# First expert stage in 64-slot tiles on quarters of the matrix array, its expert weights loaded in nine blocks each

## The chip, the core and the metric

The kernel runs on one NeuronCore of a Trainium2 chip. The core has TensorE (PE in the profile) for matrix products, VectorE (DVE), ScalarE (ACT), GpSimd (POOL) and SyncE (SP). In this kernel SP issues all plain transfers, and POOL issues the indirect ones (gather and scatter by row number). All run side by side and wait for each other through semaphores. The metric is the device time in microseconds (us), as the median of several runs.

## What is computed

A small vision tower over 16 images of 36 tokens, so 576 tokens of width 192, in float32. Patches are normalised and projected to tokens; then come an attention block, a first mixture of experts, a Mamba-style block with its own feed-forward part, and a second mixture of experts (top 2 of 8). The change is in the first mixture:

```python
route = softmax(x @ router_w + router_b)          # 576 tokens, 8 experts
max_prob, max_ind = route.max(), route.argmax()   # every token goes to one expert
for e in range(8):                                # w1, w2: 192x512   w3: 512x192
    oe = silu(xe @ w1[e]) * (xe @ w2[e]) @ w3[e]  # xe: the tokens of expert e
out = out.bfloat16 * max_prob
```

## The kernel before, in words

**Tiles of slots.** Tokens are sorted by expert on the chip. A tile is 128 slots that all belong to one expert. 576 tokens over 8 experts can need at most (576 + 8*127) // 128 = 12 tiles, so the program always runs 12 (`M1_TILES`). Tiles 0 to 7 are the first tile of experts 0 to 7; tiles 8 to 11 are the overflow, and belong to the expert that a table `te` names, which VectorE computes after routing. Each tile has its own weights: `wup` (w1 and w2, with the 192 input rows cut into 128 and 64) and `wdn` (w3). There are 8 weight buffers (`M1_BUFS`) for the first stage and 6 larger ones, in the same memory, for the second.

**Loading.** `expert_weights` on SP issues five transfers per tile: 96x1024, 32x1024, 64x512 and 64x512 elements into `wup`, 128x768 into `wdn` (lines 417 to 421). Experts 0 to 5 are issued during attention, then the token rows are written out (`token_rows`), then experts 6 and 7 and `later_experts` for the overflow tiles. Tile 8 waits for `v_te` and for the first tile's end (`p_y` counts the tiles finished by the down product), tile 9 for the second tile's end, and so on. For an overflow tile SP reads the expert number with `value_load` (line 440) and computes each source address.

**Computing.** For tile j TensorE runs `up_main` (K=128 rows of input: 8 products of 128x128x128, line 1604), `up_rest` (the remaining 64 input rows: 8 products in pairs, one on the upper and one on the lower half of the array's rows, line 1616), then `down(j-1)` (4 products of 128x128x192, line 1629). ScalarE applies silu (line 774), VectorE multiplies (line 1196), ScalarE copies the result (`result`, line 781), and POOL scatters it to `token_y` (line 604). Tokens come in by POOL's gather (`xg`, line 597) and are transposed on TensorE (line 1580). Only the first tile needs no gather: `first_tile` (line 1547) selects its tokens with a product by a 0/1 matrix. Next come `sources`, which finds the row numbers, and the gathers.

**After the stage.** SP waits for all scatters (line 445), then reads `yg` back, and VectorE adds it to `h`. The next block depends on this, so the end of the stage sets the start of all that follows.

## Time and profile before

| | before |
|---|---|
| time, median of 3 runs (lowest to highest) | 406.29 us (405.89 to 407.03) |
| profiled execution: its own time, its span | 409.78 us, 408.0 us |
| PE busy | 348.6 us (85%) |
| first expert stage, first up product to last down product | 119.5 to 180.2 us |
| TensorE products of the stage | 12 tiles of 20 |
| experts loaded during the stage | 4 (of 1,152 KB each) |

How to read it: times in the trace are us from the start of the span. A row of the chain of work is start, duration, engine and line, with the number of instructions. A timeline row is start, duration, engine, line, operation and operands, with the idle time before it in brackets. PE rows count two records for each float32 product of the program (8 products are "x16"), PEld is the weight load that goes with each, and "64*64" is the rows and columns of the array used. A row of the table of windows is the stretch, its length, then busy time and count for PE, PEld, DVE, ACT and POOL (only PE and PEld where one line was asked for), the granted TensorE clock (1.00 is 2.4 GHz, 0.50 is 1.2 GHz), the busy share of the DMA engines, and GB/s. "SPq" is a transfer being issued on SP; "us to landing" runs from issue to the last byte.

### The profile page before, as it was taken

Reading aid. Unit: us, or ns where it says so; the run is one execution under the profiler, and the core shown is the slowest. Engines: PE = TensorE matmul, PEld = TensorE weight load, DVE = VectorE, ACT = ScalarE, POOL = GpSimd, SP = SyncE. Lnnn points to the kernel's source line nnn. Section 1 sums busy time; section 2 is a strip of 40 time slices with the busy share of each in tenths; the row PEclk is TensorE's granted clock in tenths of the full one; section 3 lists DMA queues with packets and bytes.
Section 4 is the critical chain, followed back from the end, with each engine's and each line's share of the span. In section 5 each row is a group of like instructions: output and inputs, shape, how many; then the busy total and the mean of one; then the engine's idle time right before and its main releaser. Section 6 shows DMA issues by size and latency. Waiting matters only on the chain.

```text
span 408.0 us, 7081 instructions
## 1 busy us (share of the span) xinstructions
PE 348.6 (85%) x2758; PEld 291.5 (71%) x2758; DVE 184.0 (45%) x474; ACT 134.8 (33%) x278; POOL 104.5 (26%) x133
## 2 busy tenths in 40 slices
PE   4999946989788999966896987888899999999970
PEld 1999923567667999962465654575799999999960
DVE  2786793996552222216398555266422212121213
ACT  2997311444303222321387042321321212121210
POOL 3299542000023443122032202000423232211120
PEclk9999976987776999996999798995999999999995
DMA  7933239930371795007003999002249999999204
GB/s 237 345 84 75 63 81 253 271 93 2 108 202 52 203 247 124 15 16 195 0 0 77 258 252 259 28 0 67 60 105 291 277 254 255 258 251 249 65 31 130
DMA packets 28707, 59.51 MB, mean 146 GB/s; under 512 B 10081, under 2 KB 15234, under 8 KB 28674
## 3 DMA queue, kind: packets, MB, share of 16 engines
q1 hardware_dynamic: 26274, 53.48, 50.1%
q0 software_dynamic: 2400, 5.57, 5.0%
q8 instruction: 22, 0.36, 0.4%
q14 instruction: 11, 0.09, 0.1%
HBM read 55.12 MB, written 3.92 MB: 145 GB/s over the span
## 4 chain that ended last, share of the span: by engine, by line
PE 60%; DVE 17%; ACT 8%; DMA 8%; issue 4%; SPq 2%; POOL 0%; DVEq 0%; POOLq 0%; ACTq 0%
PE ps L1604 15%; PE ps L1629 12%; PE ps L1616 9%; PE ps L1412 4%; PE ps L1345 4%; DMA xw<-in_xw 3%; DVE cv L1264 3%; ACT xp L661 2%; PE ps L1418 2%; DVE xn L974 2%; DVE xn L950 2%; PE ps L1467 2%; SPq L349 2%; PE ps L1547 2%; DMA yg<-token_y 2%
## 5 line engine op out<-in xcount | busy, mean ns | idle before, releaser
L1604 PE MATMUL ps<-xgt,wup 128*128 128x128 f32 x576 | 70.9, 280 | 2.3 <-DVE ht L1196 1.8
L1604 PEld LDWEIGHTS ps<-xgt,wup 128*128 128x128 f32 x576 | 69.4, 196 | 2.8 <-issue 2.8
L1196 DVE TENSOR_TENSOR ht<-sg,ps 128x384 f32<-128x384 f32 (+1 forms) x56 | 27.7, 497 | 77.5 <-ACT sg L774 75.5
L597 POOL DMA_INDIRECT xg<-token_x,src_id x26 | 25.3, 972 | 145.5 <-DVE src_id L1166 95.3
L1629 PE MATMUL ps<-wdn,ht 128*128 128x192 f32 x288 | 53.8, 335 | 0.0
L1345 PE MATMUL ps<-busy 128*128 128x512 bf16 x108 | 38.9, 486 | 11.1 <-DVE h L1211 6.6
L1629 PEld LDWEIGHTS ps<-wdn,ht 128*128 128x128 f32 x288 | 46.1, 190 | 3.1
L604 POOL DMA_INDIRECT token_y<-ysb,row_id x28 | 27.5, 981 | 67.6 <-ACT ysb L781 67.6
L774 ACT ACTIVATE sg<-ps 128x384 f32<-128x384 f32 (+1 forms) x56 | 24.8, 444 | 49.9 <-PE ps L1616 49.1
L1353 PE MATMUL ps<-weff,xp 128*128 128x193 f32 x240 | 39.9, 327 | 1.6 <-ACT xp L661 1.6
L1353 PEld LDWEIGHTS ps<-weff,xp 128*128 128x128 f32 x240 | 39.2, 190 | 2.4 <-issue 2.4
L1616 PE MATMUL ps<-xgt,wup 64*128 64x128 f32 x576 | 40.5, 286 | 0.0
L1616 PEld LDWEIGHTS ps<-xgt,wup 64*128 64x128 f32 x576 | 35.0, 190 | 4.2 <-issue 2.5
L1190 DVE COPY xgt<-ps 128x256 f32<-128x256 f32 (+1 forms) x14 | 5.7, 405 | 49.2 <-PE ps L1580 49.2
L1345 PEld LDWEIGHTS ps<-busy 128*128 128x128 bf16 x108 | 11.9, 116 | 22.2 <-issue 8.3
L661 ACT COPY xp<-xw 128x576 f32<-128x576 f32 x24 | 16.0, 667 | 6.7 <-DMA xw<-in_xw 6.7
L770 ACT COPY xgt<-ps 128x256 f32<-128x256 f32 (+1 forms) x14 | 5.0, 357 | 38.4 <-PE ps L1580 38.4
L1388 PE MATMUL ps<-ident,xn 128*128 128x128 f32 x30 | 6.3, 301 | 10.9 <-DVE xn L950 8.9
L690 ACT ACTIVATE std<-mv,eps_t 128x1 f32<-128x1 f32 x20 | 5.9, 294 | 28.4 <-DVE mv L960 28.4
L1388 PEld LDWEIGHTS ps<-ident,xn 128*128 128x128 f32 x30 | 3.9, 149 | 15.0 <-DVE xn L950 10.6
L781 ACT COPY ysb<-ps 128x192 f32<-128x192 f32 x16 | 5.1, 318 | 26.3 <-PE ps L1629 26.3
L909 DVE TENSOR_REDUCE acc<-wall 128x192 f32<-128x3072 f32 (+1 forms) x2 | 10.5, 5236 | 5.3 <-ACT wall L674 3.8
(295 smaller groups left out, 511.0 us busy)
## 6 DMA issues: line engine op xcount, KB each, us to landing
wup<-in_m_w SPq DMA_DIRECT2D x16, 576.0 KB, 8.5
wup<-in_m_w SPq DMA_DIRECT2D x48, 192.0 KB, 9.4
wdn<-in_m_w SPq DMA_DIRECT2D x16, 576.0 KB, 11.4
wup<-in_m_w SPq DMA_DIRECT2D x12, 384.0 KB, 6.1
wup<-in_m_w SPq DMA_DIRECT2D x36, 128.0 KB, 6.6
wdn<-in_m_w SPq DMA_DIRECT2D x12, 384.0 KB, 9.3
xw<-in_xw SPq DMA_DIRECT2D x2, 784.0 KB, 12.3
wall<-in_w_sh SPq DMA_DIRECT2D x2, 768.0 KB, 10.2
```

The lines of the kernel that those rows point to most:

```text
L597: g.indirect_dma_start(xg[:, j, :], None, token_x[m], bass.IndirectOffsetOnAxis(ap=src_id[:, j:j + 1], axis=0))\
L604: g.indirect_dma_start(token_y[m], bass.IndirectOffsetOnAxis(ap=row_id[:, j:j + 1], axis=0), ysb[m][:, j % 2, :], None).then_inc(d_y[j % 2 ...
L661: a.copy(xp[:, n % RING, 0:T].rearrange("p (b r x) -> p b r x", r=GRID, x=GRID), img[:, :, wy:wy + GRID, wx:wx + GRID]).then_inc(S["a_xp"], 1)
L774: a.activation(sg[:, s, 0:half], ps[:, 2 * s, 0:half], ACT.Silu).then_inc(S["a_sg"], 1)
L1196: v.tensor_tensor(ht[:, j % 2, s, 0:half], sg[:, s, 0:half], ps[:, 2 * s + 1, 0:half], ALU.mult)\
L1264: v.scalar_tensor_tensor(out=cv[:, r], in0=xpad[:, r, :, k:k + NTOK], scalar=convw[:, r, k:k + 1], in1=cv[:, r], op0=ALU.mult, op1=ALU.add ...
L1345: mm(ps[:, bank, :], busy[:, 0:P], busy[:], start=True, stop=True)
L1353: return mm(ps[:, TILE_BANK[t], 0:D + 1], xp[:, n % RING, t * P:t * P + P], weff[:, n, 0:D + 1], start=(n == 0), stop=(n == NCH - 1))
L1412: mm(outs[v][b], w[:, 0, c0:c1], moving(v, b), start=True, stop=False)
L1604: mm(ps[:, 2 * s + g, c * P:c * P + P], up[:, col:col + P], xgt[:, 0, j * P:j * P + P], start=(c == 0), stop=False)
L1616: ins = mm(ps[:, 2 * s + g, c * P:c * P + P], up[rows, col:col + P], xgt[rows, 1, j * P:j * P + P], start=False, stop=(c == tiles - 1))
L1629: ins = mm(ps[:, 4 + j % 2, 0:D], ht[:, j % 2, c // tiles, c % tiles * P:c % tiles * P + P], dn[:, c, :], start=(c == 0), stop=(c == 2 * t ...
```

## The change

Lines of the changed kernel differ; L437 and L438 are the weight loads, L1737 the up product, L1756 the down product, L1713 the transposes.

- A tile of the first stage is now 64 slots. At most (576 + 8*63) // 64 = 16 such tiles (`M1_HALVES`) are needed. Two of them, with two experts, form a pair of 128 slots; there are 8 pairs (`M1_TILES` is now 8). A gather, a silu call's size (128x256), a result and a scatter stay at 128 slots.
- Every product uses one quarter (64x64) of the array. `g` picks the row half (w1 or w2; in the down product the halves of the hidden rows), `i` the column half. The 192 input rows are three blocks of 64 (`KB`). One tile's up product is 4*3*2*2 = 48 products of 64x64x64, a pair's down product 16 of 64x64x192, a pair's transposes 12.
- The two row halves of the down product land in banks 4 and 5, so ScalarE copies one (`y_low`) and VectorE adds the other (`both_rows`).
- Each 64-slot tile has its own weights: 16 loads of an expert instead of 12, in 9 transfers instead of 5 (four blocks of 64 rows and four of 32 rows, each 512 wide, and `wdn`). There are 9 buffers instead of 8. Tile 8 now waits for `v_te` alone; tiles 9 and 10 wait for pair 0, tiles 11 and 12 for pair 1, and so on.
- `first_tile` computes its result twice, once for each column half, in three blocks: 30 products of 64 columns instead of 10 of 128.
- The second expert stage keeps its tiles and its five transfers.

```diff
-M1_TILES = (T + E * (P - 1)) // P
+H = 64
+M1_HALVES = (T + E * (H - 1)) // H
+M1_TILES = (M1_HALVES + 1) // 2
+KB = D // H
...
-M1_BUFS, M2_BUFS = 8, 6
-W_LOADS = 5
+M1_BUFS, M2_BUFS = 9, 6
+W_LOADS = (9, 5)
...
+                if m == 0:
+                    pieces = []
+                    for g in range(2):
+                        at, n = H * g, slice(g * hid, (g + 1) * hid)
+                        pieces += [(up[at:at + H, 0:hid], w12[0:H, 0, n]),
+                                   (up[at:at + DH - H, hid:2 * hid], w12[H:DH, 0, n]),
+                                   (up[at + DH - H:at + H, hid:2 * hid], w12[0:lo, 1, n]),
+                                   (up[at:at + H, 2 * hid:3 * hid], w12[lo:DH, 1, n])]
+                else:
+                    pieces = ((up[0:DH, 0:2 * hid], w12[:, 0, :]),
+                              (up[DH:P, 0:2 * hid], w12[0:lo, 1, :]),
+                              (up[0:REM, 2 * hid:3 * hid], w12[lo:DH, 1, 0:hid]),
+                              (up[REM:P, 2 * hid:3 * hid], w12[lo:DH, 1, hid:2 * hid]))
+                for dst, src in pieces:
+                    sp.dma_start(dst, src).then_inc(S[f"d_wb{b}"], 16)
                 sp.dma_start(down[:], w3).then_inc(S[f"d_wb{b}"], 16)
...
-                for j in range(first, r["n"]):
+                for j in range(first, M1_HALVES if m == 0 else r["n"]):
                     if j == E:
                         sp.wait_ge(S["v_te"], m + 1)
-                    sp.wait_ge(S["p_y"], j - r["bufs"] + 1 + r["before"])
+                    last = j - r["bufs"]
+                    if last >= 0:
+                        sp.wait_ge(S["p_y"], (last // 2 if m == 0 else last) + 1 + r["before"])
...
-                    pool.wait_ge(S["a_y"], j + 1 + before)
+                    pool.wait_ge(S["v_y" if m == 0 else "a_y"], j + 1)
...
+                if m == 0:
+                    first = ps[:, 6, 0:KB * P].rearrange("p (k t n) -> p t k n", k=KB, t=2)
+                    a.copy(xh[:, 0], first[:, 0]).then_inc(S["a_gt"], 1)
+                    a.copy(xh[:, 1], first[:, 1]).then_inc(S["a_f1"], 1)
+                    for j in range(n):
+                        silu(j, 0)
+                        if j >= 1:
+                            result(j - 1)
+                        if j + 1 < n:
+                            gathered(j + 1)
+                        silu(j, 1)
...
-                link(v.tensor_scalar(over_e[:], ps[:, 7, TT * E:TT * E + E], (P - 1) / 2 - P, 0.0,
+                link(v.tensor_scalar(over_e[:], ps[:, 7, TT * E:TT * E + E], (L - 1) / 2 - L, 0.0,
                                      ALU.add, ALU.max))
-                link(v.tensor_scalar(over_e[:], over_e[:], 1.0 / P, MAGIC, ALU.mult, ALU.add))
+                link(v.tensor_scalar(over_e[:], over_e[:], 1.0 / L, MAGIC, ALU.mult, ALU.add))
...
+                def both_rows(j):
+
+                    dve.wait_ge(S["a_yh"], j + 1)
+                    if j >= 2:
+                        dve.wait_ge(d_y[j % 2], j // 2 * 16)
+                    v.tensor_tensor(ysb[m][:, j % 2, :], y_low[:], ps[:, 5, 0:D], ALU.add).then_inc(S["v_y"], 1)
+
                 for j in range(n):
+                    if m == 0:
+                        product(j, 0)
+                        if j >= 1:
+                            both_rows(j - 1)
+                        if j + 1 < n:
+                            gathered(j + 1)
...
+                        if m_ == 0:
+                            for c in range(KB):
+                                for i in range(2):
+                                    ins = mm(ps[H * i:H * i + H, 6, c * P:c * P + P], xn[0:k, t, H * c:H * c + H],
+                                             one_first[0:k, t, :], start=(t == 0 and c == 0),
+                                             stop=(t == TT - 1 and c == KB - 1))
+                            continue
...
+                def up_half(j, s):
+
+
+
+                    t = 2 * j + s
+                    up = wbuf[0][t % M1_BUFS][0].rearrange("p (k n) -> p k n", k=KB)
+                    b, loads = weight_loads(0, t)
+                    pe.wait_ge(S[f"d_wb{b}"], loads)
+                    if s == 0:
+                        pe.wait_ge(S["a_gt"], j + 1)
+                    else:
+                        pe.wait_ge(S["a_f1" if j == 0 else "v_gt"], max(j, 1))
+                    if j >= 1:
+                        pe.wait_ge(S["v_ht"], 2 * (j - 1) + s + 1)
+                    for c in range(hid // P):
+                        for k in range(KB):
+                            for g in range(2):
+                                rows = slice(H * g, H * g + H)
+                                for i in range(2):
+                                    col = c * P + H * i
+                                    ins = mm(ps[H * i:H * i + H, 2 * s + g, c * H:c * H + H], up[rows, k, col:col + H],
+                                             xh[rows, t, k, :], start=(k == 0), stop=(k == KB - 1))
+                    ins.then_inc(S["p_gu"], 1)
+
+                def down_pair(j):
+
+
+
+                    pe.wait_ge(S["v_ht"], 2 * j + 2)
+                    if j >= 1:
+                        pe.wait_ge(S["a_yh"], j)
+                        pe.wait_ge(S["v_y"], j)
+                    else:
+                        pe.wait_ge(S["v_id"], 1)
+                    for c in range(hid // P):
+                        for g in range(2):
+                            rows = slice(H * g, H * g + H)
+                            for i in range(2):
+                                dn = wbuf[0][(2 * j + i) % M1_BUFS][1]
+                                ins = mm(ps[H * i:H * i + H, 4 + g, 0:D], ht[rows, j % 2, i, c * H:c * H + H],
+                                         dn[rows, c, :], start=(c == 0), stop=(c == hid // P - 1))
+                    ins.then_inc(S["p_y"], 1)
+
+                if m_ == 0:
+                    for j in range(n):
+                        up_half(j, 0)
+                        if j >= 1:
+                            down_pair(j - 1)
+                        if j + 1 < n:
+                            across(j + 1)
+                        up_half(j, 1)
+                    down_pair(n - 1)
+                    return
```

On TensorE, in the middle of the first expert stage, before: tiles 3 and 4 (`wup_3`, `wup_4` are weight buffers 3 and 4).

```order
L1604 MATMUL ps<-xgt,wup_3 128x128 x8
L1580 MATMUL ps<-ident,xg 128x128 x4
L1616 MATMUL ps<-xgt,wup_3 128x128 x8
L1629 MATMUL ps<-wdn_2,ht 128x192 x4
L1604 MATMUL ps<-xgt,wup_4 128x128 x8
L1616 MATMUL ps<-xgt,wup_4 128x128 x8
L1629 MATMUL ps<-wdn_3,ht 128x192 x4
```

The same place after the change (tile 3 ends pair 1, tile 4 begins pair 2; the down product alternates between the two tiles' `wdn`, 16 rows in all).

```order
L1756 MATMUL ps<-wdn_0,ht 64x192
L1756 MATMUL ps<-wdn_1,ht 64x192
L1713 MATMUL ps<-ident,xg 64x64 x12
L1737 MATMUL ps<-xgt,wup_3 64x64 x48
L1737 MATMUL ps<-xgt,wup_4 64x64 x48
L1756 MATMUL ps<-wdn_2,ht 64x192
L1756 MATMUL ps<-wdn_3,ht 64x192
```

Two tiles of 128 slots took 40 products and 4 transposes on the whole array or its row halves. Two tiles of 64 slots now take 96 up products, 16 down products and 12 transposes, all on quarters.

On SP, one overflow tile of the stage before (tile 10, into buffer 2): ISA rows compute a source address.

```order
L440 ISA x2
L417 ISA
L417 DMA wup_2<-in_m_w 96x1024
L418 ISA
L418 DMA wup_2<-in_m_w 32x1024
L419 ISA
L419 DMA wup_2<-in_m_w 64x512
L420 ISA
L420 DMA wup_2<-in_m_w 64x512
L421 ISA
L421 DMA wdn_2<-in_m_w 128x768
L440 TENSOR_LOAD te
```

And after it (tile 9, into buffer 0): its first half, which the second half repeats before the row of `wdn`.

```order
L459 ISA x2
L437 ISA
L437 DMA wup_0<-in_m_w 64x512
L437 ISA
L437 DMA wup_0<-in_m_w 32x512
L437 ISA
L437 DMA wup_0<-in_m_w 32x512
L437 ISA
L437 DMA wup_0<-in_m_w 64x512
```

SP now issues nine transfers with nine address computations for each overflow tile, and there are 8 overflow tiles instead of 4.

On TensorE, at the start of the stage, before: the warming products, the first tile's selection, the row numbers.

```order
L1345 MATMUL ps<-busy 128x512 x5
L1547 MATMUL ps<-one_first,xn 128x128 x10
L1563 MATMUL ps<-val_n,at_r 128x12
```

After:

```order
L1406 MATMUL ps<-busy 128x512 x5
L1610 MATMUL ps<-one_first,xn 64x128 x30
L1632 MATMUL ps<-val_n,at_r 128x8
```

The row numbers and thus all gathers still stand behind the selection, which is now 30 products.

## Rows read from the trace of the kernel before

**Rows 1.** The page: length, and the chain that ended last, by engine.

```profile
span 408.0 us, 7081 instructions
PE 60%; DVE 17%; ACT 8%; DMA 8%; issue 4%; SPq 2%; POOL 0%; DVEq 0%; POOLq 0%; ACTq 0%
```

**Rows 2.** Table of windows: start of the stage, and its loading phase.

```profile
119.00:131.00 12.00, 9.09 (x58) 8.17 (x60) 2.71 (x12) 2.98 (x7) 4.99 (x5) 0.72 0.21 63
139.00:157.00 18.00, 18.00 (x167) 16.94 (x166) 4.21 (x10) 5.08 (x14) 7.47 (x9) 1.00 1.02 248
```

**Rows 3.** Chain of work in the first expert stage.

```profile
114.69 3.75 PE ps L1547 x20
...
119.51 3.75 DMA xg<-token_x,src_id
...
125.26 0.39 ACT sg L774
...
126.24 3.75 PE ps L1604 x16
...
130.84 1.09 PE ps L1616 x16
...
133.43 1.78 PE ps L1604 x16
...
136.31 1.50 PE ps L1629 x8
...
177.42 2.81 PE ps L1629 x16
180.25 0.33 ACT ysb L781
```

**Rows 4.** Timeline: products on parts of the array, elsewhere in the kernel.

```profile
218.36 1.13 PE L1686 MATMUL ps<-ct,bt 64*64 64x36 f32 x32
...
231.11 1.35 PE L1712 MATMUL ps<-mix,dtx 128*64 128x72 f32 x36
```

**Rows 5.** Table of windows at these two places, all engines.

```profile
218.35:219.30 0.95, 0.95 (x33) 0.94 (x32) 0.92 (x2) 0.00 (x0) 0.00 (x0) 1.00 0.00 0
231.10:232.50 1.40, 1.40 (x38) 1.31 (x38) 0.67 (x2) 0.00 (x0) 0.00 (x0) 1.00 0.98 214
```

**Rows 6.** Timeline of SP: overflow tiles 9 and 10.

```profile
138.59 0.33 SPq L417 DMA_DIRECT2D wup<-in_m_w  x1
139.10 0.32 SPq L418 DMA_DIRECT2D wup<-in_m_w  x1
139.60 0.48 SPq L419 DMA_DIRECT2D wup<-in_m_w  x1
140.26 0.47 SPq L420 DMA_DIRECT2D wup<-in_m_w  x1
...
145.68 0.45 SPq L421 DMA_DIRECT2D wdn<-in_m_w  x1
```

**Rows 7.** Timeline of SP: one expert loaded without a table look-up.

```profile
68.54 0.47 SPq L419 DMA_DIRECT2D wup<-in_m_w  x1
69.06 0.60 SPq L420 DMA_DIRECT2D wup<-in_m_w  x1
69.69 0.58 SPq L421 DMA_DIRECT2D wdn<-in_m_w  x1
```

**Rows 8.** Transfers issued from 133.5 to 137 (tile 8): size, landing.

```profile
wup<-in_m_w SPq DMA_DIRECT2D x1, 384.0 KB, 3.4
wup<-in_m_w SPq DMA_DIRECT2D x3, 128.0 KB, 3.4
wdn<-in_m_w SPq DMA_DIRECT2D x1, 384.0 KB, 7.5
```

**Rows 9.** Transfers issued from 56 to 60 (the first expert): landing.

```profile
wdn<-in_m_w SPq DMA_DIRECT2D x1, 384.0 KB, 5.0
```

**Rows 10.** Timeline of VectorE: the table of overflow experts.

```profile
120.26 0.42 DVE L1184 TENSOR_SCALAR te<-tef 1x4 int32<-1x4 f32 x1
```

More of the change, by code:

```diff
@@ L322, in build, with weight_loads @@
         RESTS = [0, len(MOE[0]["groups"]) - 1]
-        def weight_uses(m, j):
+        def weight_loads(m, j):
             b = j % MOE[m]["bufs"]
-            uses = j // MOE[m]["bufs"] + 1
+            loads = W_LOADS[m] * (j // MOE[m]["bufs"] + 1)
             if m == 1:
-                uses += len(range(b, M1_TILES, M1_BUFS))
-            return b, uses
+                loads += W_LOADS[0] * len(range(b, M1_HALVES, M1_BUFS))
+            return b, 16 * loads
         def rows_gathered(m, i):
@@ L783, in experts @@
                 act.wait_ge(S["p_gt"], 2 * GROUPS[m] + 2)
-                a.copy(xgt[:, 0, 0:P], ps[:, 6, 0:P]).then_inc(S["a_gt"], 1)
-                for i in range(2):
-                    a.copy(xgt[REM * i:REM * i + REM, 1, 0:P], ps[REM:P, 7, 0:P]).then_inc(S["a_f1"], 1)
-                for j in range(n):
-                    if j == 0:
-                        gathered(1)
-                    elif j % 2 == 1 and j + 1 < n:
-                        gathered(j // 2 + 2)
-                    silu(j, 0)
-                    silu(j, 1)
-                    if j >= 1:
-                        result(j - 1)
+                if m == 0:
+                    first = ps[:, 6, 0:KB * P].rearrange("p (k t n) -> p t k n", k=KB, t=2)
[9 more added lines that the diff above has]
+                else:
+                    a.copy(xgt[:, 0, 0:P], ps[:, 6, 0:P]).then_inc(S["a_gt"], 1)
+                    for i in range(2):
+                        a.copy(xgt[REM * i:REM * i + REM, 1, 0:P], ps[REM:P, 7, 0:P]).then_inc(S["a_f1"], 1)
+                    for j in range(n):
+                        if j == 0:
+                            gathered(1)
+                        elif j % 2 == 1 and j + 1 < n:
+                            gathered(j // 2 + 2)
+                        silu(j, 0)
+                        silu(j, 1)
+                        if j >= 1:
+                            result(j - 1)
                 result(n - 1)
@@ L1076, in experts @@
                 r = MOE[m]
-                n, half, before, K = r["n"], r["hid"] // 2, r["before"], r["k"]
+                n, half, before, K, L = r["n"], r["hid"] // 2, r["before"], r["k"], r["slots"]
+                over = (M1_HALVES if m == 0 else n) - E
                 i_ln = 2 if m == 0 else 5
@@ L1626, in down @@
                     if j >= 2:
-                        pe.wait_ge(S["a_y"], j + (before - 1))
+                        pe.wait_ge(S["a_y"], j - 1)
                     for c in range(2 * tiles):
@@ L1631, in down, with across @@
                     ins.then_inc(S["p_y"], 1)
+                def across(j):
+                    pe.wait_ge(S[f"d_xg{j}"], rows_gathered(0, j))
+                    pe.wait_ge(S["a_gt"], j)
+                    pe.wait_ge(S["a_f1" if j == 1 else "v_gt"], max(j - 1, 1))
+                    for c in range(KB):
+                        for s in range(2):
+                            rows = slice(H * s, H * s + H)
+                            for i in range(2):
+                                ins = mm(ps[H * i:H * i + H, 6 + s, c * H:c * H + H], xg[rows, j, H * c:H * c + H],
+                                         ident[rows, rows], start=True, stop=True)
+                    ins.then_inc(S["p_gt"], 2)
@@ L1633, in experts @@
+                if m_ == 0:
+                    for j in range(n):
+                        up_half(j, 0)
+                        if j >= 1:
+                            down_pair(j - 1)
[3 more added lines that the diff above has]
+                    down_pair(n - 1)
+                    return
                 for j in range(n):
```

65 lines of the change are left out of this document (41 added, 24 removed).

## The prediction

> **What bounds the kernel now.** I read the page first. Following the chain that ended last back from the end, PE holds 60% of the span and transfers 8% [rows 1]. So most stages are decided by TensorE, with little slack, and the question is what decides the stage that is changed. The chain inside it gives the answer: from 130.8 on it is PE without a break. A tile is 1.78 us for the main up products, 1.09 for the rest and 1.50 for the down product, 4.37 in all [rows 3]. The last down product ends at 177.42 + 2.81 = 180.2, and a copy of 0.33 follows before the scatter [rows 3]. In the windows PE is busy 18.00 of 18 us between 139 and 157, while the DMA engines move 248 GB/s at a busy share of 1.02 [rows 2]. Transfers are thus also at their limit in that stretch, but for 4 experts only, and no product waits for them. The start is different: the first gather takes 3.75 us, and 16 records that later take 1.78 us take 3.75 at 126.2, because the granted clock is at its lower level there (mean 0.72 from 119 to 131) [rows 2, 3].
>
> **TensorE after the change.** One pair of 64-slot tiles has 96 up products, 16 down products and 12 transposes, each two records: 192, 32 and 24. What a record on a quarter costs is not in the trace, but its parts are. Two row halves overlap: 16 records take 1.09 us, 68 ns each, where a whole-array record takes 1.78/16 = 111 ns [rows 3]. Two column halves overlap too: 36 records of 72 columns take 1.35 us, 75 ns for two, although 72/128 of 111 ns is already 62 for one [rows 4]; the clock is at its upper level at both places used here [rows 5]. With 64x64 and only 36 columns, 32 weight loads keep PEld busy 0.94 us at full clock, 59 ns for two [rows 5]. I take 59 ns for a group of four quarters, and 192/128 * 111 = 167 ns for a group of 192 columns. A pair is then 48 * 0.059 + 8 * 0.167 + 6 * 0.059 = 2.83 + 1.34 + 0.35 = 4.5 us. Eight pairs replace twelve tiles, so left alone the stage would shrink by some 15 us. The upper bound is that only two of four overlap: 9.0 us a pair. In between lies one record per 29 ns, which is the pace of the 32 records [rows 5]: 7.6 us.
>
> **Start of the stage.** The selection goes from 10 to 30 products, on column halves. If these overlap, it is 30 steps instead of 20. It took 3.75 us for 20 [rows 3], so the extra is between 10 * 0.111 = 1.1 (full clock, which it has by then in part) and 1.9 us; without overlap 4.5. I take 1.1. The row numbers and the gather behind it move by the same: the gather starts at 120.6 and lands at 124.4. Before that only the first tile's up product can run. After it come the transposes, the up products of tiles 1 and 2, and pair 0's down product. At the lower clock level, as before in this stretch, these are 0.7 + 2.8 + 2.8, and 1.6 for the down product as the clock rises: pair 0 is done at **132.4**. All at full clock it would be 128.9.
>
> **SP, which the change loads most.** This is the step that I hold to decide. The overflow tiles are now 8 to 15. Tile 8 needs only the table `te`, written at 120.7 [rows 10] and about 1 us later now, so its issue is over before 132.4. Tiles 9 to 15 stand behind pair 0, one after the other on one queue, and each is nine transfers. A late transfer costs SP 0.33 us (96 rows), 0.32 (32 rows after 96), 0.48 and 0.47 (64 rows), 0.45 (`wdn`); between two lie 0.18 us of address computation (139.10 + 0.32 to 139.60) [rows 6]. From the end of the releasing down product (136.31 + 1.50 = 137.81) to the first transfer at 138.59 it takes 0.78, mostly the table look-up [rows 3, 6]. A transfer that follows one of 64 rows is dearer: for the same 64-row shape 0.60 against 0.47, and 0.58 for `wdn` [rows 7]. So I take 0.32 + 0.13 = 0.45 for 32 rows after 64, and 0.32 for 32 after 32. The nine: 4 * 0.475 + 2 * 0.45 + 2 * 0.32 + 0.45 = 3.9; the eight gaps 1.4; the head 0.8. **One late expert costs SP 6.1 us.** If every block of 32 rows cost 0.32 and the head 0.7, it would be 5.8; if every block cost 0.48, 6.5. The bytes are unchanged, 384 + 3 * 128 + 384 = 1,152 KB [rows 8], 4.75 us at 248 GB/s. The issue is therefore slower than the transfer. Before, the same queue had five transfers per 4.37 us and 4 such experts, and it slept between them.
>
> The Trainium skill says otherwise ("DMA: Bandwidth & Descriptors", Issuing engines are not separate DMA queues): the time on the sequencer to initiate a transfer is "usually small relative to the DMA itself". By that rule the stage would be paced by the transfers, which is the first rival below; the row of a 64x512 block here (128 KB, 0.53 us at 248 GB/s) stands against 0.48 + 0.18 us of issue.
>
> **Sum.** 132.4 + 7 * 6.11 = 175.2 is the end of the last issue; the last `wdn` is issued 0.45 before, at 174.8. It lands 3.4 to 5.0 us later: 3.4 is a 384 KB transfer on an idle queue [rows 8], 5.0 one behind four others at full rate [rows 9]. The queue is nearly drained here, so 3.8: 178.6. Then come the up product of tile 15 (1.4), silu and product (125.26 to 126.24, 0.98 [rows 3]) and the last down product (1.34): 182.3, against 180.2. The result now goes through a copy and an addition instead of one copy of 0.33, so another 0.3. The shift is 2.1 + 0.3 = **+2.4 us**. Everything behind starts later by it and is not changed. The profiled execution, 409.8 us with a span of 408.0, would become 412.2 and 410.4; it lies 3.5 us above the median. On the median of 406.29 the forecast is **408.7 us**.
>
> At nothing I cost: the issue of experts 0 to 5 (nine transfers at about 0.5 to 0.6 each, 5 us an expert, over by 90 where the token rows are written after 107); the 15 us of PE time saved, since PE then waits for weights in every pair from the fifth on (two experts are 12.2 us, a pair 4.5 to 7.6); the wait of the addition on DVE, which runs beside the next up product. Cover gone, the addition costs 0.3 once, at the end.
>
> **Rivals.**
> - **Transfers pace the stage** (the side opposite to mine). If a block's issue is cheap, or overlaps, 7 experts take 7 * 4.75 = 33.2 us from 132.4; with 1.8 for the last landing, 167.4; with 1.4 + 0.98 + 1.34, 171.1, and 0.3: 8.8 us earlier, 397.5 us. It decides from a pace under 6.11 - 2.4/7 = 5.8 us an expert. For it: DMA was at its limit with 4 experts [rows 2]. Against it: the durations of rows 6 are of the same kind of transfer. Chance 0.14.
> - **Only two quarters run at once.** A pair is 9.0 us. From 124.4: 1.4 + 5.7 for pair 0 at the lower clock, then 7 * 5.66 + 6 * 0.7 + 8 * 2.68 + 0.98 = 66.2: 197.7, or +17.8: 424 us. For it: no row shows four at once. Against it: rows and columns overlap each by itself [rows 3, 4]. Chance 0.09.
> - **A cold end.** PE waits in each of the last pairs, so the granted clock may be at its lower level for the last up and down products: + 1.4 + 1.3, 411.4 us. It belongs to my mechanism and is the top of its range.
> - **The change hits nothing**: SP a little cheaper and pair 0 earlier cancel the rest. 5.8 us an expert is -2.2, and this is why "same" has a share.
>
> **Numbers.** My mechanism has 0.66. Its own range is 405.0 (5.8 us an expert, pair 0 by 131) to 412.5 (cold end, landing 5.0). The first rival has 0.14 and reaches from 397 to 403 according to how much of the issue is hidden, the second 0.09, the rest 0.11 is what I don't see. For 8 in 10 I take 400.5 to 413.5: it leaves out the second rival and the lower half of the first. About 0.3%, 1.2 us, is what a measurement of this kernel can tell from no change. Slower by more: 0.46 of my mechanism's 0.66, the second rival, and a few hundredths, 0.57. Within: 0.17. Faster: the first rival, the low end of mine and half the rest, 0.26.
>
> **What the changed profile would show.** SP's timeline: transfers back to back from about 132 to 175, 6.1 us from one table look-up to the next. GB/s near 193 instead of 248 in that stretch. PE: idle before the up products, released by `wup` or `wdn` transfers, from the fifth pair on, and a granted clock under 1.00 there. An up half of 96 records in 1.4 us at full clock proves the four quarters, 2.8 us refutes them. The last down product ends near 182. I am wrong if SP sleeps on `p_y` between late experts, if a late expert takes SP under 5.8 us, or if PE stays busy through the stage.

## The result, and the profile after

The changed kernel takes **423.18 us** (median of 4 runs, 421.59 to 423.93). The kernel before took 406.66 us beside it (4 runs, 405.89 to 407.24). The ratio is 1.040, with a 95% interval of 1.036 to 1.044: slower. The forecast was 408.7 us, in a range of 400.5 to 413.5. The sign was right, and the size was 14.5 us short.

The profiled run took 421.59 us, with a span of 419.9. First the page: length, the queue that brings the engines' code, and the chain by engine.

```profile
span 419.9 us, 10251 instructions
...
q8 instruction: 33, 0.54, 0.5%
...
PE 48%; DVE 17%; SPq 10%; issue 7%; ACT 6%; DMA 5%; POOL 5%; DVEq 0%; POOLq 0%; ACTq 0%
```

The program has 3170 more instructions [rows 1]. "issue" on the chain grew from 4% to 7% and SP's queue from 2% to 10%. The instruction queue has 33 packets; 0.54 MB in 33 is 16 KB each. The page of before has a third fewer:

```profile
q8 instruction: 22, 0.36, 0.4%
```

The table of windows, the middle two of them beside [rows 2]. Its columns are the stretch, its length, busy time of PE, PEld, DVE, ACT and POOL, the granted clock, DMA share and GB/s.

```profile
119.00:131.00 12.00, 8.54 (x236) 7.12 (x236) 2.16 (x10) 2.52 (x5) 4.04 (x4) 0.78 0.68 187
...
139.00:157.00 18.00, 12.52 (x508) 11.64 (x508) 3.11 (x8) 2.80 (x8) 3.96 (x4) 0.91 0.74 185
157.00:176.00 19.00, 12.43 (x545) 11.74 (x548) 3.04 (x8) 2.81 (x8) 1.93 (x2) 0.91 0.58 180
```

From 139 to 157 PE was busy 18.00 of 18 us before. It is now busy 12.52, with three times the records (508 for 167). So it idles nearly a third of the time, and a pair takes 8.8 us where 4.5 was forecast (the down products of pairs 0 and 6 end 52.7 us apart). What it waited for is in the view of waits, from 120 to 196 (us in total, times, longest); PEld and PE rows tell of the same stops, once by the weight load and once by the product.

```profile
PEld ps L1737 <- issue: 20.0, 20, 2.3
PE ps L1737 <- issue: 17.2, 18, 2.2
```

For late weights the products waited 1.1 us in the whole stage. The rest is "issue", time in which it waited for nothing that the profile shows. The timeline of PE around two of these stops:

```profile
159.46 0.51 PE L1713 MATMUL ps<-ident,xg 64*64 64x64 f32 x18
162.22 0.34 PE L1713 MATMUL ps<-ident,xg 64*64 64x64 f32 x6 [2.25 <-issue]
162.35 1.99 PE L1737 MATMUL ps<-xgt,wup 64*64 64x64 f32 x121
166.49 0.33 PE L1737 MATMUL ps<-xgt,wup 64*64 64x64 f32 x6 [2.15 <-issue]
```

PE stops in the middle of a group of transposes, does 6 + 121 = 127 records, and stops again in the middle of an up half. Nothing in the program lies at these places. But 127 records with their weight loads are 254 instructions, and a packet of the instruction queue is 16 KB. The packets of that queue in the trace begin at 159.83 and 164.16, and the last records before the two stops start at 159.75 and 164.12. The packets end at 160.78 and 165.08, and PE goes on at 162.22 and 166.49, 1.4 us later each time. That holds throughout: in this trace and in three of the experiments below (two transfers, no late weights, gathers later) all 33 stops of over 0.8 us put down to "issue" after the first up half end 1.2 to 1.6 us after a packet does. In this stage there are 15 such packets after, and 5 before. **TensorE waits for its own code.**

Six of the 15 cost it less than 0.4 us or nothing. Five of these (from 128.87, 133.17, 142.23, 168.30 and 185.88) came wholly or in part while the granted clock was at its lower level, where the records follow each other at some 27 ns instead of 15: a slower PE is hardly held up.

Now the chain of work in the stage: one late expert on SP's queue, then the end of the stage.

```profile
136.57 0.48 SPq L437
137.23 0.93 SPq L437
138.34 0.32 SPq L437
...
140.21 0.43 SPq L437
...
141.18 0.33 SPq L437
141.69 0.51 SPq L437
142.39 1.37 SPq L438
...
185.54 3.92 DMA wdn<-in_m_w
189.51 0.92 PE ps L1737 x46
...
190.78 1.00 PE ps L1737 x48
191.80 0.39 ACT sg L796
192.22 0.43 DVE ht L1240
192.69 1.57 PE ps L1756 x32
194.29 0.33 ACT y_low L804
194.64 0.37 DVE ysb L1248
```

The chain runs through SP from 135.8 to 185.5 without a break, as forecast: nine transfers an expert, no sleep between them. Most have the forecast durations (0.48, 0.32, 0.43). Two do not: 0.93 at 137.23 and 1.37 at 142.39. Packets of the instruction queue are under way from 136.65 to 137.80 and from 142.23 to 143.39. All nine transfers of over 0.75 us between 136 and 186 begin during such a packet, and each of the nine ends 0.36 to 0.37 us after the packet does (137.23 + 0.93 = 138.16, 142.39 + 1.37 = 143.76). So SP's queue is held until TensorE's code has come. Not every packet does that: during those of 150.71 and 164.16 transfers were issued at the usual 0.45 to 0.48 us.

The last down product ends at 194.26, before at 180.24 [rows 3]: +14.0 us. The span grew by 11.9 only, because everything behind the stage took 2.2 us less than in the profile of before (225.6 us after it, 227.8 before; eight of the nine other profiles of this study lie within 1 us of the 225.6). That leaves +14 us of the 16.5 between the medians to the stage, and the rest to single runs that differ by 1 to 3 us.

### The profile page after: what moved, and what is told of

Its sections match the earlier page's. It is cut to its first block, busy times and chain, and to the rows that moved or that the text cites. A ratio compares the mean times of both kernels' runs of the same rounds, so it can differ in the third digit from the quotient of the medians.

```text
span 419.9 us, 10251 instructions
## 1 busy us (share of the span) xinstructions
PE 334.9 (80%) x4256; PEld 280.7 (67%) x4256; DVE 183.5 (44%) x475; ACT 130.4 (31%) x266; POOL 96.5 (23%) x125
## 3 DMA queue, kind: packets, MB, share of 16 engines
HBM read 59.31 MB, written 3.72 MB: 150 GB/s over the span
## 4 chain that ended last, share of the span: by engine, by line
PE 48%; DVE 17%; SPq 10%; issue 7%; ACT 6%; DMA 5%; POOL 5%; DVEq 0%; POOLq 0%; ACTq 0%
PE ps L1673 10%; PE ps L1698 8%; SPq L437 8%; PE ps L1685 5%; PE ps L1473 4%; DVE cv L1325 3%; PE ps L1737 3%; PE ps L1406 2%; PE ps L1479 2%; DVE xn L1013 2%; DVE xn L989 2%; DMA yg<-token_y 2%; PE ps L1610 2%; PE ps L1528 1%; SPq L438 1%
## 5 line engine op out<-in xcount | busy, mean ns | idle before, releaser
L1737 PE MATMUL ps<-xgt,wup 64*64 64x64 f32 x1536 | 34.1, 237 | 18.6 <-issue 17.2
L1673 PE MATMUL ps<-xgt,wup 128*128 128x128 f32 x384 | 45.6, 275 | 1.2 <-DVE ht L1240 1.2
L1673 PEld LDWEIGHTS ps<-xgt,wup 128*128 128x128 f32 x384 | 44.8, 192 | 1.4 <-issue 1.4
L1737 PEld LDWEIGHTS ps<-xgt,wup 64*64 64x64 f32 x1536 | 30.4, 149 | 22.0 <-issue 20.0
L623 POOL DMA_INDIRECT token_y<-ysb,row_id x24 | 23.5, 981 | 85.9 <-ACT ysb L808 44.1
L1698 PE MATMUL ps<-wdn,ht 128*128 128x192 f32 x192 | 35.2, 334 | 0.0
L1698 PEld LDWEIGHTS ps<-wdn,ht 128*128 128x128 f32 x192 | 30.8, 190 | 1.8
L1685 PE MATMUL ps<-xgt,wup 64*128 64x128 f32 x384 | 25.7, 280 | 0.0
L1685 PEld LDWEIGHTS ps<-xgt,wup 64*128 64x128 f32 x384 | 22.7, 187 | 2.3 <-issue 1.3
L1756 PE MATMUL ps<-wdn,ht 64*64 64x192 f32 x256 | 15.9, 389 | 0.9 <-DVE ht L1240 0.9
```

Source lines behind the costliest of these rows:

```text
L623: g.indirect_dma_start(token_y[m], bass.IndirectOffsetOnAxis(ap=row_id[:, j:j + 1], axis=0), ysb[m][:, j % 2, :], None).then_inc(d_y[j % 2 ...
L1673: mm(ps[:, 2 * s + g, c * P:c * P + P], up[:, col:col + P], xgt[:, 0, j * P:j * P + P], start=(c == 0), stop=False)
L1685: ins = mm(ps[:, 2 * s + g, c * P:c * P + P], up[rows, col:col + P], xgt[rows, 1, j * P:j * P + P], start=False, stop=(c == tiles - 1))
L1698: ins = mm(ps[:, 4 + j % 2, 0:D], ht[:, j % 2, c // tiles, c % tiles * P:c % tiles * P + P], dn[:, c, :], start=(c == 0), stop=(c == 2 * t ...
L1737: ins = mm(ps[H * i:H * i + H, 2 * s + g, c * H:c * H + H], up[rows, k, col:col + H], xh[rows, t, k, :], start=(k == 0), stop=(k == KB - 1))
```

## The experiments

Three theories stand at the start. **Code:** TensorE's instructions don't arrive fast enough, 127 records to a packet, and the stops between packets pace the stage. **SP:** the nine transfers an expert pace it, and the stops only fill time in which PE would have waited. **Array:** quarters are slower than thought.

**Two transfers an expert instead of nine.** The host lays out each expert's up weights as the buffer holds them. TensorE's program is that of the changed kernel.

```diff
-W_LOADS = (9, 5)
+W_LOADS = (2, 5)
-                    pieces = []
-                    for g in range(2):
-                        ...
+                    pieces = ((up[:], w12),)
```

> The changed kernel, with the first stage's weights laid out by the host so that an expert comes in two transfers (128x1536 and 128x768) instead of nine; TensorE's work is untouched. Theory SP (my forecast's: the queue that issues the weights paces the stage): with two transfers a late expert costs SP some 2 us instead of 7.2, so the stage falls back to transfers or TensorE at 4.5 us a pair, and its last down product ends near 170 instead of 194; time about 398 us. Theory code (TensorE waits for its own instructions: in the changed trace its gaps put down to issue come every 127 records, together with a 16 KB fetch of code, 2 to 2.5 us each): TensorE already takes 8.3 to 9.5 us a pair where all weights are there, so the stage ends only by the last waits earlier, near 190; time 417 to 421 us.

Measured: 416.72 us, ratio 1.018 (1.013 to 1.023). One of its four runs took 1738 us and is left out of the ratio. SP now needs 1.6 to 2.1 us an expert and sleeps in between. The waits of PE in the stage:

```profile
PEld ps L1731 <- issue: 11.9, 7, 2.8
PEld ps L1707 <- issue: 7.9, 3, 4.4
```

The stops are still there, fewer but longer, up to 4.4 us. In that longest one PE ran dry at 136.99, the packet began only at 138.91 and ended at 139.88, and PE went on at 141.27. Three packets (from 148.58, 152.09 and 167.72) passed without a stop at the lower clock, though one at that level (from 145.03) cost 2.6 us. With SP's burden gone the kernel is still slower than before. SP alone is not the cause; in this test it is worth 6.5 us.

**Fewer products, nine transfers.** One up product uses both column halves, so the up products of a pair have 96 records instead of 192.

```diff
-                                for i in range(2):
-                                    col = c * P + H * i
-                                    ins = mm(ps[H * i:H * i + H, 2 * s + g, c * H:c * H + H], up[rows, k, col:col + H],
-                                             xh[rows, t, k, :], start=(k == 0), stop=(k == KB - 1))
+                                ins = mm(ps[:, 2 * s + g, c * H:c * H + H], up[rows, k, c * P:c * P + P],
+                                         xh[rows, t, k, :], start=(k == 0), stop=(k == KB - 1))
```

> The changed kernel with nine transfers, but the up product is made on row halves only (64x128x64): 24 products a tile instead of 48, the same numbers in the same places. A pair then has 152 records instead of 248. Theory SP in its plain form: nothing on SP's queue is changed, a late expert stays at 7.2 us, the end stays near 194, time 422 to 424. Theory code: the gaps come every 127 records, so half as many, TensorE needs about 96 * 0.056 + 1.3 + 0.6 = 7.3 us a pair, and SP, whose long transfers (0.8 to 1.85 instead of 0.47 us) in the changed trace begin during a fetch of TensorE's code, comes down from 7.2 to 6.1 to 6.7 us an expert: the stage ends 4 to 8 us earlier, time 415 to 419.

Measured: 429.92 us (422.39 to 440.35); with such a spread no ratio is given, and the profiled run is the lowest. The windows:

```profile
135.00:150.00 15.00, 15.00 (x168) 13.92 (x170) 1.66 (x5) 1.79 (x5) 1.95 (x2) 0.50 0.41 121
...
165.00:180.00 15.00, 15.00 (x314) 14.58 (x314) 2.93 (x8) 2.81 (x8) 1.93 (x2) 1.00 0.68 194
```

The stops are gone (0.3 us of "issue" in the stage), and PE is busy all the time. At full clock a pair takes 7.3 us, against 8.8 on average in the changed kernel. But a half now costs 2.62 us at full clock where quarters need 1.40, and up to about 154 the clock was granted at half (1.2 GHz), at which it costs 4.97. So this run mixes two things: it removes the stops and pays for wider records at a lower clock. It supports code against array (quarters do overlap four at a time), and says nothing about the total. One more thing can be read from it: with nine packets of code in the stage instead of 15, a late expert costs SP 6.7 us ((185.29 - 138.29) / 7) instead of 7.2, with nothing changed on its queue.

**Both together.**

> Both edits together: two transfers an expert and the up product on row halves. Theory SP: as with two transfers alone, but with TensorE at 7.3 us a pair, the stage ends near 120 + 8 * 7.3 = 180; time about 407. Theory code: the same number, since neither limit is left: 405 to 411. If it stays above 415, something that neither names is at work.

Measured: 408.94 us (12 runs, 405.53 to 430.4), ratio 1.002 (0.997 to 1.007): as fast as before. At full clock a pair takes 7.3 us, and eight of them are no shorter than the twelve tiles of before. Its profile shows a run of 426 us in which the clock was granted at half from about 155 on, so only the stretch before it is used here. The two edits together bring the time back, and two transfers alone do not. Whether wide columns alone would do so at full clock is not shown: in their run one pair took 13.8 us at the lower clock instead of 7.3. That SP and TensorE's code were two nearly equal limits is read from the changed kernel, whose chain runs through SP while PE waits for weights only 1.1 us.

**The kernel before with nine transfers an expert.** This measures the disputed price of SP by itself, without quarters.

```diff
-W_LOADS = 5
+W_LOADS = (9, 5)
+                if m == 0:
+                    for g in range(2):
+                        n = slice(g * hid, (g + 1) * hid)
+                        pieces += [(up[0:64, n], w12[0:64, 0, n]), (up[64:DH, n], w12[64:DH, 0, n]),
+                                   (up[DH:P, n], w12[0:lo, 1, n]),
+                                   (up[REM * g:REM * g + REM, 2 * hid:3 * hid], w12[lo:DH, 1, n])]
```

> The kernel before with one part of the change: the first stage's weights in nine transfers of 64 and 32 rows by 512, TensorE's work untouched. A late expert should cost SP 6.1 us (my term) if the extra in the changed kernel (7.2) comes from TensorE's code fetches, and 7.2 if it is the price of nine transfers as such. Both theories: four late experts at 6 to 7 us from 133.5 are all there before tile 11 is due at 173, so the time stays at 406.5 +- 1.

Measured: 408.72 us (10 runs, 405.75 to 410.22), ratio 1.002 (0.998 to 1.007). The timeline of SP for a late expert:

```profile
136.01 4.77 SPq L430 DMA_DIRECT2D wup<-in_m_w  x8
140.96 0.45 SPq L431 DMA_DIRECT2D wdn<-in_m_w  x1
142.20 2.96 SPq L430 DMA_DIRECT2D wup<-in_m_w  x5
```

From one expert to the next it is 6.2 us (136.01 to 142.20). The three late experts of which the whole is seen take 6.1 to 6.4 from the look-up to the last transfer. The price of 6.1 in the forecast was right, where TensorE fetches little code (four packets from 128 to 180, against 14 from 128 to 187 in the changed kernel). In the changed kernel it was 7.17 on average: (185.98 - 135.82) / 7.

**The changed kernel without late weight traffic.** SP loads experts 0 to 8, and tiles 9 to 15 use what the buffers hold.

```diff
-                for j in range(first, M1_HALVES if m == 0 else r["n"]):
+                for j in range(first, M1_BUFS if m == 0 else r["n"]):
```

> The changed kernel without its late weight transfers: SP brings experts 0 to 8 and nothing more, and tiles 9 to 15 multiply by what the buffers still hold (left out: the weights of tiles 9 to 15, so their rows are computed with other experts' numbers). TensorE executes exactly the instructions of the changed kernel. If TensorE's own code sets its pace (a stop of about 2 us every 127 records, the rest at one record per 15 to 27 ns), pairs still take 7 to 8.5 us, the last down product ends between 183 and 190 and the time is 411 to 419 us. If the late transfers and their issue set the pace, and the stops only follow from them, pairs fall to about 4.5 us, the last down product ends near 168 and the time is near 396. In between (stops shorter because the DMA engines are idle): each stop of 1.3 us instead of 2.1 gives about 180 and 407. The first up half took 7.06 us in the changed kernel and 1.60 in the one with two transfers; here the nine transfers ahead of it are unchanged, so if they cause it, it is about 7 again.

Measured: 412.02 us (409.82 to 414.43), ratio 1.016 (1.006 to 1.026). The windows (16 DMA engines at 0.04, clock 1.00) and the waits:

```profile
150.00:165.00 15.00, 11.17 (x538) 10.34 (x538) 3.02 (x8) 2.81 (x8) 2.05 (x3) 1.00 0.04 13
```

```profile
PEld ps L1737 <- issue: 18.5, 24, 1.9
PEld ps L1713 <- issue: 3.6, 4, 1.8
```

This is the cleanest of the tests. From 136 on hardly anything is transferred, the clock is full, no product waits for a weight, and a pair still takes 7.3 us (the down products of pairs 1 and 6 are 36.6 us apart). From the first gather to the last down product the stage takes 64.6 us (117.30 to 181.92), against 60.7 before. By SP's theory it would have been about 46 (an end near 168, as expected above, from a gather at 121.7 in the changed kernel). The code theory holds. From 150 to 165 PE stands still for 3.8 of 15 us, which is 1.9 of the 7.3 us of a pair. The other 0.9 us over the forecast 4.5 lies in gaps too short for the view of waits or in the products themselves, and is not broken down. The stops are shorter here (up to 1.9 us, against 2.3 and 4.4): they come without traffic on the DMA engines, and are longer with it.

**Gathers later.** The first up half of the changed kernel took 7.06 us instead of 1.4. Here GpSimd waits for it before it gathers.

```diff
+                if m == 0:
+                    pool.wait_ge(S["p_gu"], 1)
                 for j in range(1, 1 + AHEAD):
                     gather(j)
```

> The changed kernel, but GpSimd waits for the first up half (96 products) before it issues its first four gathers. In the changed kernel that half took 7.06 us, in pieces of 2 to 10 records between gaps of about 0.65 us, while four gathers ran one after the other (121.73 to 126.68); without the late transfers it was the same, 117.4 to 123. If GpSimd's indirect transfers starve TensorE of code, the half now takes 1.5 to 2.5 us, the starvation moves behind it to whatever runs beside the gathers, and the time falls by 1 to 4 us to 419 to 422. If the nine transfers per expert or anything else causes it, the half still takes 5 to 7 us and the time rises by the later gathers, to 424 to 428.

Measured: 422.10 us (419.12 to 424.85), ratio 1.036 (1.028 to 1.045). The timeline of PE in the changed kernel, part of the first half:

```profile
123.01 0.40 PE L1737 MATMUL ps<-xgt,wup 64*64 64x64 f32 x10 [0.40 <-issue]
123.80 0.34 PE L1737 MATMUL ps<-xgt,wup 64*64 64x64 f32 x4 [0.38 <-issue]
124.53 0.34 PE L1737 MATMUL ps<-xgt,wup 64*64 64x64 f32 x3 [0.39 <-issue]
```

and with the gathers later:

```profile
119.40 1.75 PE L1739 MATMUL ps<-xgt,wup 64*64 64x64 f32 x96
122.07 1.20 POOL L616 DMA_INDIRECT xg<-token_x,src_id  x1 [59.16 <-PE ps L1739]
...
127.20 0.92 PE L1715 MATMUL ps<-ident,xg 64*64 64x64 f32 x24 [6.05 <-DMA xg<-token_x,src_id]
```

The half takes 1.53 us from its first record to its last. So the gathers starve TensorE of records: 3 to 10 at a time, with 0.4 to 1.1 us between. It is not the wait for a packet of code, since none is under way between 119.73 and 128.87 in the changed kernel. In the kernel without late weights, whose gathers start at the same point of the program, the half took 6.99 us. It needs a second condition. With two transfers an expert the same half took 1.60 us although a gather ran beside it. The time does not fall: the gathers come late now, and the transposes of pair 1 wait 6.05 us for them. The start of the stage is thus bound by both.

**The matrices as the moving operand.** If records are the price, the way out is fewer of them. Tokens are loaded as weights (64 slots on a quarter) and the experts' matrices move: 12 up products of 512 columns a pair instead of 96 of 64. The hidden rows then need 4 transposes (`ident`) before the down product. Two transfers an expert, with the host layout of the first experiment; a buffer's up part is reloaded once its up products are done.

```diff
+                    for k in range(KB):
+                        for g in range(2):
+                            rows = slice(H * g, H * g + H)
+                            for i in range(2):
+                                up = wbuf[0][(2 * j + i) % M1_BUFS][0].rearrange("p (k n) -> p k n", k=KB)
+                                ins = mm(ps[H * i:H * i + H, 2 * (j % 2) + g, :], xh[rows, 2 * j + i, k, :],
+                                         up[rows, k, :], start=(k == 0), stop=(k == KB - 1))
+                    ins.then_inc(S["p_gu"], 2)
...
+                    for c in range(hid // P):
+                        ins = nc.tensor.transpose(ps[:, 7, c * P:c * P + P], hs[j % 2][:, c * P:c * P + P], ident[:])
```

> 64-slot tiles on 64x64 quarters with the tokens as weights and the experts' matrices as the moving operand: 12 up products 64x64x512, 6 transposes of gathered rows, 4 transposes of the hidden rows and 8 down products a pair, some 60 to 72 TensorE records instead of 248, and two transfers per expert, whose up part is reloaded as soon as a pair's up products are done. If four quarters overlap and a record costs by its columns (0.111 us for 128), the up products of a pair take 12 * 2 / 4 * 0.444 = 2.7 us, the pair 5.2 to 5.5 us, the last down product ends near 170 and the time is 395 to 399 us. The code theory wants no stop in this stage longer than one per two pairs, since 127 records are now two pairs; it gives at most 8 us more, if each such stop is 2 us. If instead the transfers are the limit (4.75 us an expert at 248 GB/s, 7 experts from about 128), the last weights land near 163 and nothing changes in the sum. If the quarters did not overlap with 512 moving columns, the up products alone would be 10.7 us a pair and the time about 440.

Measured: **395.25 us** (394.26 to 395.44), ratio 0.972 (0.963 to 0.981). It beats both kernels. One pair on the timeline:

```profile
130.90 2.81 PE L1735 MATMUL ps<-wup,xgt 64*64 64x512 f32 x24
133.64 0.66 PE L1743 MATMUL ps<-ident,ht 128*128 128x128 f32 x4
134.23 0.88 PE L1716 MATMUL ps<-ident,xg 128*64 128x128 f32 x12
135.08 1.52 PE L1756 MATMUL ps<-wdn,ht 128*64 128x192 f32 x16
136.53 2.81 PE L1735 MATMUL ps<-wup,xgt 64*64 64x512 f32 x24
```

56 records a pair instead of 248, 5.63 us from one to the next (130.90 to 136.53), and PE busy 17.00 of 17 us from 128 to 145 while the DMA engines move 356 GB/s. The stage takes 47.4 us (120.29 to 167.65). The instruction queue has 4 packets in it instead of 15, and no product waits for code.

The Trainium skill has this form ("TensorEngine Tiling (Array Packing)", When to Use Tiling) as swapping the stationary and the streaming operand, and under Instruction Overhead it warns against taking the tiling factor from a dimension that is already small. The runs agree with the advice, but not for the page's reason, which is a fixed cost of each product: here quarters with 64 moving columns overlap as they should (58 ns for four records) and stop for code every 127 records, and those with 512 don't.

**The same with nine transfers an expert**, once with two late experts loaded together, once with one after the other:

```diff
-            for js in ((8,), (9, 10), (11, 12), (13, 14), (15,)):
+            for js in [(j,) for j in range(8, 16)]:
```

> The same kernel as m1_moving with the nine plain transfers of 64 and 32 rows per expert. Now the queue's issue is the only burden left: TensorE has 60 to 72 records a pair, so its code hardly stops anything. If one late expert costs SP 6.1 us when TensorE fetches little code, tiles 9 to 15 take 42.7 us from about 128.5, the last transfer lands near 175, the last down product ends at 177 to 180, and the time is 404 to 407 us; SP shows no wait for buffers between late experts. If the 7.2 us per expert of the changed kernel belong to the nine transfers themselves, it is 128.5 + 50.4 + 3.8 = 182.7, last down product 185, time about 412. If issue overlapped with anything and the transfers' bytes set the pace, it is that of m1_moving.

> m2_moving_nine with one late expert after the other (its eight up blocks, then its down block) instead of two at a time. In m2_moving_nine the seven last experts took SP 44.2 us (6.3 each), as the prediction priced them, but the last down product ended 14 us after the last issue, because the pair before last got its weights together with half of the next pair and started 7 us late, and three down parts then ran in series. If that order was the whole of it, the last issue ends near 171, its transfer lands near 175, the up and down products of the last pair take about 6.5 us more, the stage takes 62 to 64 us from the first gather to the last down product (60.4 in the kernel before, 68.2 in m2_moving_nine), and the time is 408 to 411 us: the prediction's own mechanism with its own price. If a queue of nine transfers costs more in some way that the issue times don't show, it stays at 413 to 416.

Measured: 414.99 us (413.79 to 417.16), ratio 1.020 (1.011 to 1.030), and 414.79 us (414.11 to 416.57), ratio 1.021 (1.016 to 1.027). They are 8 and 4 us above the top of what I expected. SP's price of an expert is not the reason: in the first it took 44.2 us for seven experts (6.3 each), in the second the last six took 6.1 to 6.8. The timeline of SP and then the chain, from the second run (its "issue" of 5.86 us is PE waiting for the last weights; no packet of code is near it):

```profile
137.30 0.36 SPq L449 DMA_DIRECT2D wdn<-in_m_w  x1
138.43 4.72 SPq L447 DMA_DIRECT2D wup<-in_m_w  x8
...
170.05 4.71 SPq L447 DMA_DIRECT2D wup<-in_m_w  x8
174.95 0.44 SPq L449 DMA_DIRECT2D wdn<-in_m_w  x1
```

```profile
172.49 5.86 issue
178.35 4.60 PE ps L1741 x24
182.95 0.60 PE ps L1749 x4
...
184.32 1.52 PE ps L1762 x16
185.84 0.60 PE ps L1749 x4
...
187.21 1.54 PE ps L1762 x16
```

Two terms were wrong. Tile 9's `wdn` can only be issued when pair 0's down product is done, and in this kernel that is at 137.1, since it stands behind pair 1's up products. My sum had the release at 128.5. And from the landing of the last weights (PE starts at 178.35) it is 10.4 us to the end, because up, transposes, copy and down of two pairs follow in series and the clock had fallen in the wait (the up products take 4.60 us instead of 2.73). I had put 6.5 there. My explanation of the first run, that two experts together were to blame, is not borne out: one by one is no faster, though in that run pair 0 also ended later (137.1, against 131.5). What the pair shows is the price of nine transfers: without code stops it is 414.99 - 395.25 = 19.7 us on this kernel, measured side by side.

## Why the prediction was wrong, by its own steps

- **"A pair is then 4.5 us": the step that failed**, and with it the 15 us of PE time that I took as spare. It stood at nothing in the sum, and it came in by the terms below, SP's price above all. The array does what I said: 96 records of a half start within 1.40 us, 58 ns for a group of four [rows 5], so the rival "only two quarters at once" is refuted, although its 424 us happened to be the time. What I left out is that records must first arrive. A pair of 248 records takes 7.3 us without late weights, and 8.8 in the changed kernel. The reading of one record per 29 ns [rows 5], which I set aside, gives 7.6 us a pair and comes near by chance: between the stops the records come 15 ns apart at full clock, and it is the stops that cost.
- **Pair 0 done at 132.4.** Measured 135.8. The selection took 6.34 us (+2.6, not +1.1): its column halves overlap, but every step cost 0.21 us at half clock, where I had taken 0.11 for the added ten, and 24 of 30 came before the clock rose. The first up half took 7.06 us beside the gathers and was over at 128.3, while the first gather was to land at 124.4: +3.9, and what follows took 0.5 less. The later selection is hidden in it. Together: +3.4 us.
- **One late expert costs SP 6.1 us.** Right by itself: 6.1 to 6.4 in the kernel before with nine transfers. In the changed kernel 7.17, because nine transfers that begin during a packet of the instruction queue take 0.8 to 1.9 us instead of 0.47, 6.4 us more in all. Seven times 1.06 is +7.4 us, the largest part of the miss, and it is a side effect of the step that failed: the term left out is what 248 records a pair do to the queue beside them.
- **The last `wdn` lands 3.8 later.** 3.92: right.
- **The last pair, 3.72 us.** 4.75 (189.51 to 194.26), since the half, with a stop of 0.35 us in it, took 2.3 us instead of 1.4: +1.0.
- **Sum.** 3.4 + 7.4 + 0.1 + 1.0 = 11.9, and 182.3 + 11.9 = 194.2; measured 194.26. The +0.3 for the addition was 0.37.
- **The rival "transfers pace the stage"** is refuted twice: nine transfers cost 6.1 us or more wherever measured, while two cost 1.6 to 2.1 and move the same bytes. The moving form comes out near this rival's time, 395.3 us against 397.5, but for another reason: there PE is busy all through the loading, and the transfers don't pace it.
- **The cold end.** Not there: the clock was at its lower level from about 185 to 188.3, before the last weights landed, and the last up half and down product (189.51 on) ran at the upper one. The mean of 0.87 from 183 to 196 hides that.

The Trainium skill ("Runtime: NRT & Kernel Launch", Instruction fetch mechanics) says that an engine's code comes in blocks of 16 KB on a queue of the engine's own, and that crossing a block is "mostly hidden". The traces agree on the block: 33 packets in 0.54 MB. They disagree on the hiding where records are short and dense. In this stage nine of the 15 crossings cost 0.9 to 2.3 us with weight traffic beside them, and one cost up to 4.4 with two large transfers an expert. In the moving form, where 127 records last over 10 us, it costs nothing.

**Left open.** The stops are made up of a late start of the packet (up to 2 us after PE ran dry), the packet itself (0.9 to 1.6) and 1.2 to 1.6 us until PE goes on. Why the last part is there, why a packet starts late, and why it holds up some of SP's issues and not others, no run tells. Which second condition lets a gather starve TensorE is not known. And why the clock stayed at half up to about 154 in the kernel with wide columns, with PE busy nearly all that time, was not tried.

## What to carry to other kernels

Count instructions as well as cycles: here a product of 64 moving columns on a quarter of the array finished in less time than its code takes to arrive, and four times the parallelism became a slower stage; give quarters long moving operands (512 columns: 5.63 us a pair instead of 7.3). When a change adds both records to TensorE and transfers to a queue, look for a second limit right behind the first, and cost the two together: here two transfers an expert alone left the kernel 1.8% behind, and together with fewer records they made it level. A transfer's price on its queue (0.32 to 0.60 us and 0.18 between two) is paid per transfer and not per byte (0.34 us for 768 KB in the run with two transfers, 0.48 for 128 KB here), so ask the host for a layout that needs few.

## What the runs showed of the hardware that I had not expected

- At full clock TensorE stops every 127 records of this kind (254 instructions with their weight loads), mostly for 0.9 to 2.3 us, and up to 4.4 us in the kernel with two transfers an expert. It goes on 1.2 to 1.6 us after the 16 KB packet has come. At the lower clock, with records some 27 ns apart instead of 15, the packets of the changed kernel held it up for less than 0.4 us each; one in the kernel with two transfers cost 2.6 us.
- Four gathers by GpSimd, one behind the other, cut a half of 96 records into pieces of 3 to 10 and stretched it from 1.53 to 7.06 us.
- SP's issue of a transfer that takes 0.47 us took 0.79 to 1.85 us nine times when it began during a packet of TensorE's code, and ended 0.36 to 0.37 us after the packet. Some issues during a packet were not held.
- On quarters, a product with 512 moving columns costs 0.43 us for a group of four at full clock: the overlap of four holds at that length too.
